# Second graph layer of a four-stage network on one core: slots per tile in place of the extra gathers

## The chip, the cores and the metric

One core of one Trainium2 chip runs the whole program. The metric is the device time of the program in microseconds, as the median of several executions. TensorE does matrix products, VectorE, ScalarE and GpSimd do elementwise work, SyncE issues transfers. In the profile they are PE (with PEld for its weight loads), DVE, ACT, POOL and SP.

## The reference, cut to what matters

The program is a graph layer, an expert layer, a second graph layer and a second expert layer over 3125 nodes of 256 features. The change concerns the sum over edges of the second graph layer. There are 103,125 edges, sorted by destination (`dst`), with a relation number each:

```python
h_src = h_hc[src]
r_uv = r_hc[edge_type]
m = clifford_linear(h_src * r_uv, msg_w, msg_b)
m = m * gate[:, :, None]
m = m * norm[:, None, None]
h_agg = jax.ops.segment_sum(m, dst, num_segments=num_nodes)
h_out = clifford_linear(h_hc + h_agg, upd_w, upd_b)
```

The linear map is taken out of the sum, so that the kernel sums products of a node's row and a relation's row, `h[src] * r[edge_type]`, over the edges of each destination. A 257th column carries the term of the bias.

## The kernel before, in words

**Tiles, blocks and halves.** The 3125 nodes lie in 25 tiles of 128 (`NT`). The sorted edges are cut into 404 blocks (`BLOCKS`) of two halves of 128 edges, 808 halves (`HALVES`). Each half is added to the tile in which its first edge lies. A half that begins in one tile and ends in a later one leaves out the edges behind the border. For these there are 24 extra halves (`EDGES_AT`), one for each tile from the second on, in 12 further blocks: the half in which that tile's first edge lies, this time with the weights of that tile. So `total` is 416 rounds.

**The loop, `aggregate` (lines 598 to 721).** Each engine runs over n from 0 to 415, and semaphores alone set the order:
- SyncE (L644) loads the 256 relation rows of block n into slot n mod 12 of `agg_r_rel` (`SLOTS` is 12). For the 12 extra rounds it reads two starts from the table `b_start` (L646) and loads 128 rows from each (L650).
- GpSimd (L659) gathers the 256 node rows with two indirect transfers of 128 rows into slot n mod 12 of `agg_r_rows`, by the table of sources `b_src`. It waits first until the sums of block n-12 are done, which used that slot (L656).
- ScalarE (L626, L629) makes a one-hot matrix per half from the distance of each edge's node to the tile's first (`b_near`).
- VectorE (L697) multiplies the gathered rows of both halves with the relation rows, in place. Then `add(n)` (L680 to L688) adds the two sums of block n-2 (`LAG` is 2) to the accumulator's tiles, whose numbers it reads from the table `b_tile` (L677). After each addition it waits for the one before (L686).
- TensorE (L715) multiplies each half's one-hot with its 128 x 257 products into one of six banks of PSUM, and counts `s_sum` up after the second. It waits for the product of round n, for the one-hot, and for the additions of block n-3, which free its banks.
- `beside` puts small work of the layer's end between the rounds, every 14th: transposes (L2512), a matmul (L2518), a copy by ScalarE (L2533) and two additions by VectorE (L2545, L2547).

`s_sum` begins at 13, from matmuls on zeros (L707), so that the waits of the first rounds pass. `s_sum >= n + 2` thus says that the sums of block n-12 are done.

**Tables.** `edge_blocks` (L436 to L578) makes `b_start`, `b_tile`, `b_src` and `b_near` at the start of the program and stores them. For the extra halves `b_start` holds the first edge of the half, a multiple of 128.

**The tile buffer.** `c.xn` (L2599, 25 x 256 numbers per partition) holds the normalised rows of each expert layer. It is free during `aggregate`.

## Time and profile before

| | us |
|---|---|
| median of 3 runs | 3672.89 |
| lowest and highest of the runs | 3659.75, 3688.53 |
| the profiled execution's own time | 3648.6 |
| its span, first to last instruction | 3646.8 |
| first gather to last addition of `aggregate` | 1873.9 to 3089.4 |

A row of the profile names the line, the engine, the operation and output<-inputs; then how often, and the time in us. "Idle before" is how long the engine had nothing to do before that row, with what ended it. "issue" stands for no wait that the profile shows, "remote" for an event that comes from no instruction or transfer of the profile. In a timeline a row begins with its start and its length in us from the span's start. The granted clock of TensorE is 1.0 at 2.4 GHz and 0.5 at 1.2 GHz.

### The profile page before, as it was taken

Reading aid. Unit: us, or ns where it says so; the run is one execution under the profiler, and the core shown is the slowest. Engines: PE = TensorE matmul, PEld = TensorE weight load, DVE = VectorE, ACT = ScalarE, POOL = GpSimd, SP = SyncE. Lnnn points to the kernel's source line nnn. Section 1 sums busy time; section 2 is a strip of 40 time slices with the busy share of each in tenths; the row PEclk is TensorE's granted clock in tenths of the full one; section 3 lists DMA queues with packets and bytes.
Section 4 is the critical chain, followed back from the end, with each engine's and each line's share of the span. In section 5 each row is a group of like instructions: output and inputs, shape, how many; then the busy total and the mean of one; then the engine's idle time right before and its main releaser. Section 6 shows DMA issues by size and latency. Waiting matters only on the chain. (4 is left out here: it accounts for less than half of the span.)

```text
span 3646.8 us, 47855 instructions
## 1 busy us (share of the span) xinstructions
PE 2327.2 (64%) x11533; PEld 1741.3 (48%) x11533; DVE 1680.2 (46%) x4536; ACT 1447.2 (40%) x3766; POOL 1987.8 (55%) x1945
## 2 busy tenths in 40 slices
PE   1658888957877745787115445544654455589997
PEld 1235556635555534666104233333333333579996
DVE  5656777735554623000455455544654555621110
ACT  0345556524443422222145334333433333345553
POOL 2546566555556457554537776776777765023332
PEclk9978999979978857999657767776766767799999
DMA  6646565555656565457346666666666664264232
GB/s 231 198 123 180 170 182 173 155 185 191 200 176 206 167 204 181 153 163 234 89 126 193 183 181 189 190 179 173 198 185 173 188 183 134 86 215 117 47 84 60
DMA packets 366569, 605.80 MB, mean 166 GB/s; under 512 B 82338, under 2 KB 235179, under 8 KB 363536
## 3 DMA queue, kind: packets, MB, share of 16 engines
q1 hardware_dynamic: 261984, 331.36, 28.2%
q0 software_dynamic: 100208, 265.56, 27.4%
q10 hardware_dynamic: 4144, 6.20, 0.5%
q8 instruction: 95, 1.56, 0.2%
q14 instruction: 138, 1.13, 0.1%
HBM read 443.45 MB, written 164.32 MB: 167 GB/s over the span
## 5 line engine op out<-in xcount | busy, mean ns | idle before, releaser
L659 POOL DMA_INDIRECT agg_r_rows<-h_table,parts_and_x x832 | 861.0, 1035 | 393.9 <-issue 232.5
L715 PE MATMUL agg_r_sums<-agg_r_rows,agg_r_onehot 128*128 128x257 f32 x1664 | 580.3, 493 | 598.2 <-issue 300.0
L715 PEld LDWEIGHTS agg_r_sums<-agg_r_rows,agg_r_onehot 128*128 128x128 f32 x1664 | 371.0, 241 | 794.4 <-issue 549.5
L688 DVE TENSOR_TENSOR acc<-acc,agg_r_sums 128x257 f32 (+1 forms) x836 | 353.6, 423 | 541.7 <-remote 347.4
L626 ACT ACTIVATE agg_r_gap<-iota,parts_and_x 128x128 f32<-128x128 f32 x832 | 286.0, 391 | 571.5 <-remote 330.2
L1558 POOL DMA_INDIRECT rl_buf<-r_table,kinds x312 | 336.2, 1078 | 247.7 <-DMA relation_rows<-rl_buf 150.6
L1388 PE MATMUL la_acc<-la_parts,la_counts 128*128 128x512 f32 x1250 | 342.6, 432 | 95.6 <-DVE la_parts L1471 38.3
L1558 POOL DMA_INDIRECT rm_buf<-r_table,kinds x280 | 270.3, 965 | 213.6 <-DMA relation_rows<-rm_buf 111.3
L1958 PE MATMUL f_pH<-f_xT,f_w 128*128 128x128 f32 x2816 | 350.6, 282 | 39.6 <-DMA f_w<-in_L_ffn_w 14.6
L1958 PEld LDWEIGHTS f_pH<-f_xT,f_w 128*128 128x128 f32 x2816 | 335.5, 196 | 72.5 <-issue 41.9
L1977 PE MATMUL f_pY<-f_w,f_hT 128*128 128x256 f32 x1408 | 333.5, 387 | 32.1 <-DMA f_w<-in_L_ffn_w 22.0
L1388 PEld LDWEIGHTS la_acc<-la_parts,la_counts 128*128 128x128 f32 x1250 | 253.0, 206 | 172.4 <-issue 84.5
L2043 ACT ACTIVATE f_hT<-f_pH,f_b 128x128 f32<-128x128 f32 x704 | 197.6, 372 | 333.2 <-PE f_pH L1958 332.8
L697 DVE TENSOR_TENSOR agg_r_rows<-agg_r_rows,agg_r_rel 128x514 f32<-128x514 f32 x416 | 287.8, 692 | 43.8 <-DMA agg_r_rows<-h_table,parts_and_x 32.6
L1977 PEld LDWEIGHTS f_pY<-f_w,f_hT 128*128 128x128 f32 x1408 | 262.6, 193 | 71.2 <-DMA f_w<-in_L_ffn_w 25.6
L1428 ACT ACTIVATE la_counts<-matrix 128x640 fp32r<-128x640 fp8e4 x250 | 180.9, 735 | 246.7 <-remote 98.1
L1154 PE MATMUL b_strips<-b_oh,b_at 128*128 128x400 bf16 x980 | 211.4, 349 | 93.8 <-issue 45.6
L2200 POOL DMA_INDIRECT f_xb<-xn_table,f_token x120 | 118.2, 985 | 257.7 <-DVE f_home L2148 124.8
L1275 DVE TENSOR_SCALAR b_oh<-b_numbers,b_code 128x400 bf16<-128x400 f16 x980 | 252.8, 324 | 0.0
L2188 POOL DMA_INDIRECT f_ys<-f_yb,f_home x56 | 88.2, 1575 | 270.5 <-DVE f_yb L2173 252.9
L2167 DVE TENSOR_TENSOR f_plain<-f_pY,f_b 128x256 f32<-128x256 f32 x56 | 23.8, 425 | 359.2 <-PE f_pY L1977 359.2
L629 ACT ACTIVATE agg_r_onehot<-agg_r_gap 128x256 f32<-128x256 f32 x416 | 173.3, 417 | 23.8 <-remote 8.2
(404 smaller groups left out, 3355.4 us busy)
## 6 DMA issues: line engine op xcount, KB each, us to landing
agg_r_rel<-relation_rows SPq DMA_DIRECT2D x404, 260.0 KB
relation_rows<-rl_buf SPq DMA_DIRECT2D x156, 260.0 KB
relation_rows<-rm_buf SPq DMA_DIRECT2D x140, 260.0 KB
relation_rows<-f_rr_buf POOLq DMA_DIRECT2D x60, 260.0 KB
f_w<-in_L_ffn_W SPq DMA_DIRECT2D x28, 512.0 KB
f_w<-in_L_ffn_W SPq DMA_DIRECT2D x14, 1024.0 KB
agg_r_rows<-h_table,parts_and_x POOLq DMA_INDIRECT x832
f_w<-in_L_ffn_w SPq DMA_DIRECT2D x38, 256.0 KB
```

What stands on the lines that cost most here:

```text
L626: last = nc.scalar.activation(gap[:, n % HOT, t, :], c.iota[:, 0:P], ACT.Abs, bias=c.tab["b_near"][:, bass.ds(g * 2 + t, 1)])
L659: pool.indirect_dma_start(rows[:, n % SLOTS, t, :], None, table, bass.IndirectOffsetOnAxis(ap=indices[:, t:t + 1], axis=0)).then_inc(s_row ...
L688: v.tensor_tensor(here, here, sums[:, (2 * (n - LAG) + t) % BANKS, 0:used], ALU.add).then_inc(s_acc, 1)
L697: v.tensor_tensor(here, here, rel[:, n % SLOTS, :, 0:used], ALU.mult).then_inc(s_ready, 1)
L715: last = nc.tensor.matmul(sums[:, (2 * n + t) % BANKS, 0:used], onehot[:, n % HOT, t, :], rows[:, n % SLOTS, t, 0:used], start=True, stop= ...
L1154: last = nc.tensor.matmul(strips[:, n % BANKS, 0:CODES], at[:, n % 2, t, :], oh[:, n % 2, t, :], start=t == 0, stop=t == DEEP - 1)
L1275: last = v.tensor_scalar(oh[:, n % 2, t, :], numbers[:, :], code[:, q, 1, own, t:t + 1], None, ALU.is_equal)
L1388: last = nc.tensor.matmul(acc[:, n % 2, :], counts[:, i, j, :], parts[:, s, :], start=s == 0, stop=s == NT - 1)
L1558: pool.indirect_dma_start(self.buf[:, n, g, :], None, self.table, bass.IndirectOffsetOnAxis(ap=self.c.kinds[:, at:at + 1], axis=0)).then_i ...
L1958: last = nc.tensor.matmul(pH[s][:, f * P:(f + 1) * P], w1b[:, s, f // (FC // 2), at:at + P], xT[:, s, h, :], start=h == 0, stop=h == KD - 1)
L1977: last = nc.tensor.matmul(pY[s][:, 0:D], hT[:, s, f, :], w2b[:, s, f, :], start=f == 0, stop=f == FC - 1)
L2043: nc.scalar.activation(hT[:, s, f, :], pH[s][:, f * P:(f + 1) * P], act_fn, bias=b1s[:, bass.ds(e, 1), f]).then_inc(s_hT, 1)
```

## The change

VectorE keeps each multiplied half in a slot of a new buffer, `c.saved`, that has one slot of 257 numbers for each of the 25 tiles and one spare. The slot's number is the tile of the half's first edge, so the last half that begins in a tile stays in its slot. That is the half that the extra sum of the next tile reads. The 12 extra rounds load, gather and multiply nothing. TensorE reads two table entries for each half (which half, and from `b_tile` its slot) and multiplies straight from the slot.

The copy stands in `add(n)`, ahead of each addition, and copies from the product of block n-2. So the gather's slot is free only after that copy: the limit in `gather` goes from `n + 2` to `n + 2 + BANKS // 2` (that is n + 5), the sums of block n-9. `c.xn` becomes a view of `c.saved`.

```diff
@@ tables
-                sp.dma_start(c.tab["b_start_d"], at[:, 0, :]).then_inc(s_saved, 16)
+                sp.dma_start(c.tab["b_start_d"], at[:, 1, :]).then_inc(s_saved, 16)
...
-                v.tensor_scalar(at[:, 0, :], starts, bits, bits, ALU.arith_shift_right, ALU.logical_shift_left)
@@ aggregate, SyncE
-                for n in range(BLOCKS, total):
-                    starts = [sp.value_load(c.tab["b_start"][0:1, at:at + 1], min_val=0, max_val=EDGE_TILES * P)
-                              for at in (2 * (n - BLOCKS), 2 * (n - BLOCKS) + 1)]
-                    sp.wait_ge(s_sum, n + 2)
-                    for t in range(2):
-                        sp.dma_start(rel[:, n % SLOTS, t, :], relation_rows[bass.ds(starts[t], P), :]).then_inc(s_rel[n % SLOTS], 16)
@@ GpSimd
-                    pool.wait_ge(s_sum, (n + 2))
+                    pool.wait_ge(s_sum, n + 2 + BANKS // 2)
...
-                for n in range(total):
+                for n in range(BLOCKS):
                     gather(n, c.tab["b_src"][:, n * 2:n * 2 + 2])
@@ VectorE, add(n)
                     for t in range(2):
+                        half = 2 * (n - LAG) + t
+                        if 0 <= half < HALVES:
+                            if half:
+                                dve.wait_ge(s_save, half)
+                            v.tensor_copy(saved[:, bass.ds(tiles[t], 1), :].rearrange("p a d -> p (a d)"), rows[:, (n - LAG) % SLOTS, t, 0:used])\
+                                .then_inc(s_save, 1)
                         dve.wait_ge(s_acc, 2 * n + t + BANKS)
@@ VectorE, the loop
+                    if n < BLOCKS:
-                    dve.wait_ge(s_rel[n % SLOTS], loads_of(n))
+                        dve.wait_ge(s_rel[n % SLOTS], (n // SLOTS + 1) * 16)
                         dve.wait_ge(s_rows[n % SLOTS], (n // SLOTS + 1) * 32)
                         here = rows[:, n % SLOTS, :, 0:used]
                         v.tensor_tensor(here, here, rel[:, n % SLOTS, :, 0:used], ALU.mult).then_inc(s_ready, 1)
                     add(n)
@@ TensorE
+                def slot_of(n, t):
+                    at = 2 * (n - BLOCKS) + t
+                    half = pe.value_load(c.tab["b_start"][0:1, at:at + 1], min_val=0, max_val=HALVES - 1)
+                    tile = pe.value_load(c.tab["b_tile"][0:1, bass.ds(half + 2 * LAG, 1)], min_val=0, max_val=NT)
+                    return saved[:, bass.ds(tile, 1), :].rearrange("p a d -> p (a d)")
+                def sum_up(n):
+                    terms = [rows[:, n % SLOTS, t, 0:used] if n < BLOCKS else slot_of(n, t) for t in range(2)]
                     pe.wait_ge(s_acc, 2 * (n + LAG + 1))
                     pe.wait_ge(s_oh, n + 1)
-                    pe.wait_ge(s_ready, g + 1)
+                    pe.wait_ge(s_ready, min(n + 1, BLOCKS))
+                    kept = HALVES if n >= BLOCKS else 2 * (n + 1 - BANKS // 2)
+                    if kept > 0:
+                        pe.wait_ge(s_save, kept)
                     for t in range(2):
+                        last = nc.tensor.matmul(sums[:, (2 * n + t) % BANKS, 0:used], onehot[:, n % HOT, t, :], terms[t], start=True, stop=True)
@@ build
-        c.xn = c.sb("xn", [P, NT, D])
+        c.saved = c.sb("saved", [P, (NT + 1) * (D + 1)])
+        c.xn = c.saved[:, 0:NT * D].rearrange("p (t d) -> p t d", d=D)
```

## Rows read from the trace of the kernel before

**Rows 1.** The page's costliest groups: the gathers, TensorE, VectorE in `aggregate`
```profile
L659 POOL DMA_INDIRECT agg_r_rows<-h_table,parts_and_x x832 | 861.0, 1035 | 393.9 <-issue 232.5
L715 PE MATMUL agg_r_sums<-agg_r_rows,agg_r_onehot 128*128 128x257 f32 x1664 | 580.3, 493 | 598.2 <-issue 300.0
L688 DVE TENSOR_TENSOR acc<-acc,agg_r_sums 128x257 f32 (+1 forms) x836 | 353.6, 423 | 541.7 <-remote 347.4
L697 DVE TENSOR_TENSOR agg_r_rows<-agg_r_rows,agg_r_rel 128x514 f32<-128x514 f32 x416 | 287.8, 692 | 43.8 <-DMA agg_r_rows<-h_table,parts_and_x 32.6
```

**Rows 2.** One line, L659: xcount, ns min/median/max, first and last start
```profile
L659 POOL DMA_INDIRECT agg_r_rows<-h_table,parts_and_x x832: 947/953/1463, 1873.9 to 3071.7; - x167
```

**Rows 3.** Waits of POOL in `aggregate`: us in total, times, longest
```profile
POOL agg_r_rows L659 <- issue: 232.5, 760, 0.9
POOL agg_r_rows L659 <- remote: 91.6, 43, 5.3
POOL agg_r_rows L659 <- PE agg_r_sums L707: 56.0, 1, 56.0
POOL agg_r_rows L659 <- PE agg_r_sums L715: 13.8, 28, 2.7
```

**Rows 4.** Timeline from 2402 us: quick rounds, all engines
```profile
2402.12 0.69 DVE L697 TENSOR_TENSOR agg_r_rows<-agg_r_rows,agg_r_rel 128x514 f32<-128x514 f32 x1
2402.36 1.27 POOL L659 DMA_INDIRECT agg_r_rows<-h_table,parts_and_x  x1 [0.30 <-PE agg_r_sums L715]
2402.77 0.99 DVE L688 TENSOR_TENSOR acc<-acc,agg_r_sums 128x257 f32 x2
...
2403.68 0.69 DVE L697 TENSOR_TENSOR agg_r_rows<-agg_r_rows,agg_r_rel 128x514 f32<-128x514 f32 x1
...
2403.94 1.26 POOL L659 DMA_INDIRECT agg_r_rows<-h_table,parts_and_x  x1 [0.30 <-issue]
```

**Rows 5.** Timeline of VectorE and GpSimd, 2310 to 2334 us: slow rounds
```profile
2310.65 0.69 DVE L697 TENSOR_TENSOR agg_r_rows<-agg_r_rows,agg_r_rel 128x514 f32<-128x514 f32 x1
...
2319.58 0.99 DVE L688 TENSOR_TENSOR acc<-acc,agg_r_sums 128x257 f32 x2 [8.23 <-issue]
...
2332.89 0.99 DVE L688 TENSOR_TENSOR acc<-acc,agg_r_sums 128x257 f32 x2 [11.72 <-remote]
...
2333.54 0.95 POOL L659 DMA_INDIRECT agg_r_rows<-h_table,parts_and_x  x1 [5.27 <-remote]
```

**Rows 6.** Timelines of DVE and of POOL, 110 to 124 us: one-input operations
```profile
114.91 7.27 DVE L959 TENSOR_SCALAR parts_and_x<-parts_and_x,ln_mean,ln_var 128x256 f32<-128x256 f32 x22
...
115.92 7.96 POOL L1558 DMA_INDIRECT r_buf<-r_table,kinds  x1 [0.30 <-issue]
```

**Rows 7.** Single lines L962 and L2541: a copy from SBUF, one from PSUM
```profile
L962 DVE COPY parts_and_x<-matrix x1: 281/281/281, 114.0 to 114.0; 1x256 f32<-1x256 f32 x1
...
L2541 DVE COPY g_offset<-be_result 128x256 f32<-128x256 f32 x1 | 0.4, 418 | 0.0
```

**Rows 8.** Timelines at the end of `aggregate`: last gathers, last rounds
```profile
3041.45 0.96 POOL L659 DMA_INDIRECT agg_r_rows<-h_table,parts_and_x  x1 [0.30 <-issue]
...
3071.75 0.95 POOL L659 DMA_INDIRECT agg_r_rows<-h_table,parts_and_x  x1 [0.31 <-issue]
...
3084.51 0.69 DVE L697 TENSOR_TENSOR agg_r_rows<-agg_r_rows,agg_r_rel 128x514 f32<-128x514 f32 x1
...
3085.91 0.69 DVE L697 TENSOR_TENSOR agg_r_rows<-agg_r_rows,agg_r_rel 128x514 f32<-128x514 f32 x1
3086.51 2.85 DVE L688 TENSOR_TENSOR acc<-acc,agg_r_sums 128x257 f32<-128x257 f32 x6
```

**Rows 9.** Single lines L646 and L1750: table reads by SP and by TensorE
```profile
L646 SPq TENSOR_LOAD <-parts_and_x x24: 3/268/705, 3025.6 to 3082.4; - x24
L646 SPq FUSED_REGOPS  x24: 3/152/713, 3025.9 to 3082.7; - x24
...
L1750 PEldq TENSOR_LOAD <-flags x1: 484/484/484, 1280.0 to 1280.0; - x1
L1750 PEldq FUSED_REGOPS  x1: 165/165/165, 1280.5 to 1280.5; - x1
```

More of the change, by code:

```diff
@@ L603, in aggregate @@
     total = BLOCKS + EDGES_AT // 2
+    saved = c.saved[:, :].rearrange("p (t d) -> p t d", d=used)
     with Core(nc) as k:
@@ L611, in aggregate @@
         s_rows = [c.pool_sem(f"{name}_rows{s}") for s in range(SLOTS)]
-        s_gap, s_oh, s_ready, s_sum, s_acc, s_gate = (k.sem(f"{name}_{x}") for x in (
-            "gap", "onehot", "ready", "sum", "acc", "gate"))
+        s_gap, s_oh, s_ready, s_save, s_sum, s_acc, s_gate = (k.sem(f"{name}_{x}") for x in (
+            "gap", "onehot", "ready", "save", "sum", "acc", "gate"))
         with nc.Block() as block:
@@ L667, in _ @@
                 v = nc.vector
-                def loads_of(n):
-                    slot = [q for q in range(n + 1) if q % SLOTS == n % SLOTS]
-                    return sum(16 if q < BLOCKS else 32 for q in slot)
                 def tile_of(half):
@@ L693, in _ @@
                 for n in range(total):
-                    dve.wait_ge(s_rel[n % SLOTS], loads_of(n))
-                    dve.wait_ge(s_rows[n % SLOTS], (n // SLOTS + 1) * 32)
-                    here = rows[:, n % SLOTS, :, 0:used]
-                    v.tensor_tensor(here, here, rel[:, n % SLOTS, :, 0:used], ALU.mult).then_inc(s_ready, 1)
+                    if n < BLOCKS:
+                        dve.wait_ge(s_rel[n % SLOTS], (n // SLOTS + 1) * 16)
+                        dve.wait_ge(s_rows[n % SLOTS], (n // SLOTS + 1) * 32)
+                        here = rows[:, n % SLOTS, :, 0:used]
+                        v.tensor_tensor(here, here, rel[:, n % SLOTS, :, 0:used], ALU.mult).then_inc(s_ready, 1)
                     add(n)
@@ L708, in _ @@
                 last.then_inc(s_sum, SLOTS + 1)
-                def sum_up(g, n):
-                    pe.wait_ge(s_acc, 2 * (g + LAG + 1))
-                    pe.wait_ge(s_oh, g + 1)
-                    pe.wait_ge(s_ready, g + 1)
+                def slot_of(n, t):
[5 more added lines that the diff above has]
+                    terms = [rows[:, n % SLOTS, t, 0:used] if n < BLOCKS else slot_of(n, t) for t in range(2)]
+                    pe.wait_ge(s_acc, 2 * (n + LAG + 1))
+                    pe.wait_ge(s_oh, n + 1)
+                    pe.wait_ge(s_ready, min(n + 1, BLOCKS))
+                    kept = HALVES if n >= BLOCKS else 2 * (n + 1 - BANKS // 2)
+                    if kept > 0:
+                        pe.wait_ge(s_save, kept)
                     for t in range(2):
-                        last = nc.tensor.matmul(sums[:, (2 * n + t) % BANKS, 0:used], onehot[:, n % HOT, t, :], rows[:, n % SLOTS, t, 0:used],
-                                                start=True, stop=True)
+                        last = nc.tensor.matmul(sums[:, (2 * n + t) % BANKS, 0:used], onehot[:, n % HOT, t, :], terms[t], start=True, stop=True)
                     last.then_inc(s_sum, 1)
                 for n in range(total):
-                    sum_up(n, n)
+                    sum_up(n)
                     beside.tensor(pe, n)
@@ L2598, in build @@
         crowded_gnn0(nc, c, I, edges, h_tables, x1, zh0)
-        c.xn = c.sb("xn", [P, NT, D])
+        c.saved = c.sb("xn", [P, (NT + 1) * (D + 1)])
+        c.xn = c.saved[:, 0:NT * D].rearrange("p (t d) -> p t d", d=D)
         logits = [c.sb(f"logits{q}", [P, NT, ne]) for q, ne in enumerate((E0, E1))]
```

## The prediction

> **What bounds the kernel now.** I read the page's groups first. In `aggregate` (1873.9 to 3089.4 us) no engine is full: GpSimd's gathers are busy 861.0 us, TensorE's products 580.3 us, VectorE's multiplications 287.8 us and additions 353.6 us [rows 1]. GpSimd is the nearest to full, so its waits come next. From the first gather's start to the last one's end are 3072.7 - 1873.9 = 1198.8 us [rows 2]. Of that 861.0 us are busy. The idle time is 393.9 us, of which 56.0 us lie ahead of the first gather [rows 1, 3], so 337.9 us are in the stage, and 861.0 + 337.9 is 1198.9: GpSimd's own account closes. The gap between two gathers with nothing to wait for is 0.30 us (232.5 us in 760) [rows 3]. 831 such gaps make about 252 us, which leaves 86 us of true waiting. The undisturbed gather takes 0.953 us, the median [rows 2]. 832 of them make 793 us, and the 68 us that are left are gathers that were held up.
>
> So the stage is GpSimd's: **793 + 252 + 68 held up + 86 waiting = 1199 us**, and behind it a tail of 16.7 us to the last addition (3089.4) [rows 8]. A round costs 1199 / 416 = 2.88 us, of which 2.51 us can't be had back while two gathers are made.
>
> What holds a gather up stands in the quick rounds. VectorE's round is 1.56 us (2402.12 to 2403.68). A gather that starts 0.24 us after a multiplication takes 1.27 us instead of 0.95, as if it had waited for the multiplication's end. The next starts 1.58 us later, again 0.26 us after a multiplication [rows 4]. Gathers and rounds run in step, so that nearly each gather loses 0.31 us. On the whole timeline 222 of the 416 rounds come in under 1.75 us, and 222 x 0.31 = 69 us is all of the held-up time.
>
> What makes GpSimd wait stands in the slow rounds. There VectorE stands 8 to 12 us before an addition, although the products it adds were issued long before, while GpSimd gathers on until the ring of 12 slots is full and it waits (5.27 us in the longest) [rows 5]. Just then the sums come through together. I count some 26 such endings. I can't say what delays the sums, but they cost only through GpSimd's 86 us.
>
> **The change part by part.**
>
> *The 24 gathers, 12 multiplications and 24 loads that go.* At the end GpSimd is the bound: the last gather of block 403 starts at 3041.45 and ends at 3042.4, the last of all ends at 3072.7, 24 gathers on [rows 8]. 24 x (0.953 + 0.303) = **-30 us**. The multiplications and loads lay beside that.
>
> *The 12 extra rounds are then a tail.* Before, the tail behind the last gather was 16.7 us. After it, the last gather must land and block 403 be multiplied, summed, copied and added two rounds later: some 7 us. Then come 12 rounds in which TensorE makes four table reads each. TensorE's only read in the trace took 0.484 us with 0.165 us of register work behind it; SyncE's took 0.268 and 0.152 us in the median [rows 9]. That is 0.42 to 0.65 us each, 1.7 to 2.6 us for four, one behind the other in its queue, and with the matmuls' own issue I take 2.7 us a round, near the upper row since it is the same engine. Were the reads hidden, a round would cost the 1.39 us at which the last rounds ran (3084.51 to 3085.91) [rows 8]. 7 + 12 x 2.7 + 3 for the last additions = 42 us, between 7 + 12 x 1.39 + 3 = 27 and, at 4 us a round, 58. Against 16.7 us: **+25 us** (+10 to +41).
>
> *The copies on VectorE.* 808 copies of 128 x 257. A copy of 256 numbers within SBUF took 0.281 us on one partition, one from PSUM 0.418 us [rows 7]; these are the bounds, and I take the first, since source and target are both in SBUF. With the address from a register and part of the second copy hidden in the gap between the additions, a quick round of 1.56 us becomes about 2.0 us (1.9 to 2.3). That is under the 2.51 us of two gathers, so VectorE does not become the bound: **0 us** directly. The cover is thin: a round of more than 2.5 us would put all beyond it on the path.
>
> *Gathers held up.* This decides. One row shows that VectorE's work with one input can shut a gather out: during 22 back-to-back L959 a gather took 7.96 us, until they were over [rows 6]. A copy can do that for its 0.28 us. Against it stands the lock step. If a gather that waited for a multiplication is let in at its end, it ends 0.83 us later, and the next starts at 0.69 + 0.83 + 0.30 = 1.82 us of a round that now has 2.0 us: ahead of the next multiplication. The step is broken, and gathers then meet a multiplication (0.69 us) or a copy (0.28 us) only by chance. Over 2.7 us of two gathers, that is (0.69² + 2 x 0.28²) / 2.7 = 0.24 us a round, or 404 x 0.24 = 95 us if each met part by chance alone; many fall into slow stretches without any, as now, and I take 78 us: **+10 us** (-40 if most are free; the upper bound is the first rival).
>
> The Trainium skill ("SBUF — State Buffer", section "Who interferes with whom") says that a VectorE copy in a two-port mode takes the port pair that GpSimd shares, for the whole instruction, while an operation with two SBUF inputs stops only GpSimd's reads. The trace agrees with 7.96 us under L959. By that rule every copy that meets a gather costs up to 0.28 us, 808 x 0.28 = 226 us at the very worst, where chance alone gives a tenth of it.
>
> *The shorter ring.* Gathers now wait for the sums of block n-9, not n-12. TensorE's new wait on the copies of block n-3 ends with the additions for which it waits anyway: 0 us. But three rounds of lead are gone: a slow stretch fills the ring after 3 x 2.51 = 7.5 us less. More endings, each with some 3.3 us of wait (86 / 26): between 18 and 38 of them, **+10 us** (-25 to +40).
>
> *The table, the larger buffer, one VectorE operation less* lie in other stages and off their paths: 0 us.
>
> Sum, against the profiled execution's own 3648.6 us: -30 + 25 + 10 + 10 = +15, about 3664 us. That execution stands 24 us under the median of the runs, so as a median **3688 us**.
>
> **The rivals.**
>
> *The lock step holds, at the longer round (slower).* If the first copy follows the multiplication without a gap in which a gather gets in, the gather is let in 0.94 us into the round, and the next starts at 0.94 + 0.83 + 0.30 = 2.07 us, just behind the next multiplication at 2.0. Then each gather of a quick stretch takes the whole 2.0 us, 0.74 us too much. VectorE's first addition starts 0.65 us after the multiplication's start, 0.04 us ahead of its end [rows 4], and 22 of L959 kept a gather out without letting it in between [rows 6], which speaks for it; that a wait and a register operation stand ahead of each copy speaks against. With 210 such gathers: 155 us, and 35 us by chance in the rest, against 68 now: +122 us, with the other terms (-30 + 25 + 10) +127, so 3800 us. With part of the gathers in step 3730 to 3760. It decides from the point where a round is shorter than 2.2 us.
>
> *The gathers come free (faster).* The step is broken, the quick stretches last longer, and GpSimd fills its ring more seldom: held-up time 30 us (-38), waiting 60 us (-26), tail at its lower bound (+10), gathers gone (-30): -84 us, 3590 us. For it: GpSimd with 0.95 us gathers in the slow rounds. Against: free gathers are also what leads to the full ring.
>
> *The tail and the ring alone (slower).* Table reads at 4 us a round (+41) and twice the endings (+86): with -30 and +10 that is +107, 3780 us. TensorE's single read is thin evidence, but two such misses at once are unlikely.
>
> *The change does not do what it says:* no sign of it; the slots' order and the waits cover the reads.
>
> **How the numbers follow.** My forecast (3640 to 3710) 0.43; the lock step, whole or in part, 0.32; tail and ring 0.08; gathers free 0.17. About 1% (37 us) is what a measurement here tells from no change. From the cases: faster by more 0.17, within 0.43, slower by more 0.40. The range for eight in ten is 3605 to 3800: it leaves out the far half of the free gathers and a lock step with further misses on top; the forecast's own is 3640 to 3710.
>
> **What would show it.** The gathers number 808. Median gather 0.95 us and mean 1.00 to 1.08: forecast; mean near 1.2, and timeline rows of POOL with 1.7 us at a distance of 2.0: lock step. The copy takes 0.28 us (0.42: VectorE's round passes 2.2 us, which also breaks the step). POOL's waits without the first stand under 150 us in "remote" and "PE". From the last gather to the last addition 27 to 58 us. I'm wrong if VectorE's quick round passes 2.5 us, or if the time moves outside `aggregate`.

## The result, and the profile after

The changed kernel takes 3693.19 us (median of 9 runs, 3669.74 to 3716.53), the kernel before in the same rounds 3672.89 us (3642.77 to 3698.35). The ratio is 1.0067 with a 95% interval of 1.0040 to 1.0095: 15 to 35 us more, within the 1% that was called no change. The forecast was 3688 us.

The page's costliest groups of the changed kernel, which answer to [rows 1]. The program allocates `c.saved` under the name `xn`, so `xn` in these rows is the new buffer:

```profile
L653 POOL DMA_INDIRECT agg_r_rows<-h_table,parts_and_x x808 | 791.7, 980 | 451.0 <-issue 221.3
L725 PE MATMUL agg_r_sums<-agg_r_rows,agg_r_onehot 128*128 128x257 f32 x1616 | 612.1, 528 | 550.2 <-DVE agg_r_rows L695 289.1
...
L680 DVE COPY xn<-agg_r_rows 128x257 f32 x808 | 271.2, 336 | 295.1 <-issue 217.3
L685 DVE TENSOR_TENSOR acc<-acc,agg_r_sums 128x257 f32 (+1 forms) x836 | 345.9, 414 | 110.4 <-issue 72.1
...
L695 DVE TENSOR_TENSOR agg_r_rows<-agg_r_rows,agg_r_rel 128x514 f32<-128x514 f32 x404 | 278.2, 689 | 32.1 <-issue 25.2
```

The single line of the gathers [rows 2], and GpSimd's waits in the stage [rows 3]:

```profile
L653 POOL DMA_INDIRECT agg_r_rows<-h_table,parts_and_x x808: 947/953/1474, 1890.8 to 3078.7; - x162
```

```profile
POOL agg_r_rows L653 <- issue: 221.3, 685, 3.2
POOL agg_r_rows L653 <- remote: 115.7, 50, 3.5
POOL agg_r_rows L653 <- PE agg_r_sums L725: 60.1, 72, 3.3
POOL agg_r_rows L653 <- PE agg_r_sums L705: 53.9, 1, 53.9
```

There are 24 gathers fewer, and the mean gather fell from 1035 to 980 ns: 791.7 - 808 x 0.953 leaves 22 us in which gathers were held up, where there were 68. But the idle time rose from 393.9 to 451.0 us. Without the 53.9 us ahead of the first gather and 807 gaps of 0.303 us (245 us), 153 us of true waiting are left, where there were 86. What was gained in the gathers went into waits.

A quick round is no longer in step with the gathers. The timeline of VectorE and GpSimd of the changed kernel from 2402.3 us, to be laid beside [rows 4]:

```profile
2402.30 0.69 DVE L695 TENSOR_TENSOR agg_r_rows<-agg_r_rows,agg_r_rel 128x514 f32<-128x514 f32 x1
...
2402.96 0.96 POOL L653 DMA_INDIRECT agg_r_rows<-h_table,parts_and_x  x1 [0.30 <-issue]
2402.97 0.32 DVE L680 COPY xn<-agg_r_rows 128x257 f32 x1
...
2403.21 0.41 DVE L685 TENSOR_TENSOR acc<-acc,agg_r_sums 128x257 f32 x1
...
2403.54 0.48 DVE L680 COPY xn<-agg_r_rows 128x257 f32 x1
...
2403.95 0.40 DVE L685 TENSOR_TENSOR acc<-acc,agg_r_sums 128x257 f32 x1
...
2404.22 0.95 POOL L653 DMA_INDIRECT agg_r_rows<-h_table,parts_and_x  x1 [0.30 <-issue]
2404.27 0.68 DVE L695 TENSOR_TENSOR agg_r_rows<-agg_r_rows,agg_r_rel 128x514 f32<-128x514 f32 x1
```

This round takes 1.97 us (2402.30 to 2404.27). The gathers keep their own beat of 1.26 us and run their 0.95 us.

Behind the last gather (end 3079.6 us) the 12 extra rounds are a tail, which ends with the last addition at 3131.9. The timeline of TensorE, VectorE and ScalarE in it:

```profile
3092.31 2.08 PE L725 MATMUL agg_r_sums<-xn,agg_r_onehot 128*128 x4 [3.08 <-DVE acc L685]
...
3094.43 0.88 DVE L685 TENSOR_TENSOR acc<-acc,agg_r_sums 128x257 f32<-128x257 f32 x2 [2.12 <-PE agg_r_sums L725]
...
3095.61 1.36 PEld L725 LDWEIGHTS agg_r_sums<-xn,agg_r_onehot 128*128 128x128 f32 x4 [1.94 <-issue]
3095.61 2.08 PE L725 MATMUL agg_r_sums<-xn,agg_r_onehot 128*128 x4 [1.23 <-ACT agg_r_onehot L629]
3097.73 0.69 ACT L626 ACTIVATE agg_r_gap<-iota,parts_and_x 128x128 f32<-128x128 f32 x2 [2.16 <-PE agg_r_sums L725]
3097.73 0.88 DVE L685 TENSOR_TENSOR acc<-acc,agg_r_sums 128x257 f32<-128x257 f32 x2 [2.42 <-PE agg_r_sums L725]
...
3098.91 2.07 PE L725 MATMUL agg_r_sums<-xn,agg_r_onehot 128*128 x4 [1.22 <-ACT agg_r_onehot L629]
```

The tail of 52.3 us has three parts: 12.7 us from the last gather's end to the first extra matmul (3092.31), 38.7 us of extra rounds, and 0.9 us to the end of the last addition. In the first part the five blocks still in the ring are multiplied, and at its end TensorE stands 3.08 us. In the extra rounds TensorE multiplies for 2.08 us, stands 1.23 us and multiplies again: 3.3 us a round, and VectorE and ScalarE wait for it. The rows name ScalarE's one-hot or an addition as what ended TensorE's wait. But ScalarE's last one-hot ends at 3112.1 us, and in the rounds behind it the gap is still 1.23 to 1.37 us. And the additions that TensorE waits for are those of block n-3, which are over by then. What fills the time are the table reads in TensorE's own queue, as the two single lines show (L711 reads the half, L712 the tile):

```profile
L711 PEldq TENSOR_LOAD <-parts_and_x x24: 296/300/316, 3088.3 to 3127.2; - x24
```

```profile
L712 PEldq TENSOR_LOAD <-b_tile x24: 300/305/318, 3089.1 to 3128.0; - x24
```

Lines of the same queue between 3095.7 and 3098.8 us, ahead of the round that starts at 3098.91, give their place in the round (the two reads of the half, and the register operations of the two reads of the tile):

```profile
L711 PEldq TENSOR_LOAD <-parts_and_x x2: 297/298/300, 3095.8 to 3097.2; - x2
L712 PEldq FUSED_REGOPS  x4: 46/98/151, 3096.4 to 3098.3; - x4
```

The first read starts 0.15 us after the round's first matmul (3095.61), while the matmuls run. The fourth read with its register work is over at 3098.5, and the next matmul starts 0.4 us later. So the four reads take 2.8 us with their register work, and 0.15 + 2.8 + 0.4 is the whole round. The matmuls lie beneath the reads, and the 1.23 us in which the engine stands is only what sticks out.

The stage from the first gather to the last addition, in the two profiled executions:

| | before | after | difference |
|---|---|---|---|
| gathers, undisturbed, with their gaps | 793 + 252 | 770 + 245 | -30 |
| gathers held up | 68 | 22 | -46 |
| GpSimd's waits | 86 | 153 | +67 |
| tail behind the last gather | 16.7 | 52.3 | +36 |
| stage | 1215.5 | 1241.2 | **+25.7** |

The last row is the measured loss; the rows above it are worked out with a mean gather and a mean gap and add up to it within 2 us. The profiled executions differ by more (3648.6 and 3691.8 us), and 16.9 us of it lie ahead of the stage, which starts at 1890.8 instead of 1873.9 us. That start is worth nothing here. In the profiles of the twelve experiments below it lies anywhere between 1862.9 and 1900.4 us, though ahead of the stage they differ by one small VectorE operation at most. So the runs give each kernel's time below, and the profile gives the length of the stage.

### The profile page after: what moved, and what is told of

It reads as the page before. It is cut to its first block and busy times, and to the rows that moved or that the text cites. A ratio compares the mean times of both kernels' runs of the same rounds, so it can differ in the third digit from the quotient of the medians.

```text
span 3689.9 us, 49872 instructions
## 1 busy us (share of the span) xinstructions
PE 2390.1 (65%) x11533; PEld 1769.1 (48%) x11534; DVE 1853.4 (50%) x5331; ACT 1448.0 (39%) x3766; POOL 1913.3 (52%) x1921
## 3 DMA queue, kind: packets, MB, share of 16 engines
q8 instruction: 98, 1.61, 0.2%
## 5 line engine op out<-in xcount | busy, mean ns | idle before, releaser
L653 POOL DMA_INDIRECT agg_r_rows<-h_table,parts_and_x x808 | 791.7, 980 | 451.0 <-issue 221.3
L725 PE MATMUL agg_r_sums<-agg_r_rows,agg_r_onehot 128*128 128x257 f32 x1616 | 612.1, 528 | 550.2 <-DVE agg_r_rows L695 289.1
L725 PEld LDWEIGHTS agg_r_sums<-agg_r_rows,agg_r_onehot 128*128 128x128 f32 x1616 | 381.1, 259 | 768.8 <-issue 539.7
L680 DVE COPY xn<-agg_r_rows 128x257 f32 x808 | 271.2, 336 | 295.1 <-issue 217.3
L685 DVE TENSOR_TENSOR acc<-acc,agg_r_sums 128x257 f32 (+1 forms) x836 | 345.9, 414 | 110.4 <-issue 72.1
L695 DVE TENSOR_TENSOR agg_r_rows<-agg_r_rows,agg_r_rel 128x514 f32<-128x514 f32 x404 | 278.2, 689 | 32.1 <-issue 25.2
```

Source lines behind the costliest of these rows:

```text
L653: pool.indirect_dma_start(rows[:, n % SLOTS, t, :], None, table, bass.IndirectOffsetOnAxis(ap=indices[:, t:t + 1], axis=0)).then_inc(s_row ...
L680: v.tensor_copy(saved[:, bass.ds(tiles[t], 1), :].rearrange("p a d -> p (a d)"), rows[:, (n - LAG) % SLOTS, t, 0:used])\
L685: v.tensor_tensor(here, here, sums[:, (2 * (n - LAG) + t) % BANKS, 0:used], ALU.add).then_inc(s_acc, 1)
L695: v.tensor_tensor(here, here, rel[:, n % SLOTS, :, 0:used], ALU.mult).then_inc(s_ready, 1)
L725: last = nc.tensor.matmul(sums[:, (2 * n + t) % BANKS, 0:used], onehot[:, n % HOT, t, :], terms[t], start=True, stop=True)
```

## The experiments

My first reading of the two profiles was this (theory A in the expectations): the copies break the lock step, which frees 46 us, and the shorter ring costs 67 us of waits. It was tested first.

The table has all kernels. "To the last gather" counts from the first one's start, "held up" and "waits" are worked out as above, and "quick" is the median round of those under 2.3 us, from one multiplication's start to the next. The ratio compares a kernel with runs of the kernel before that were taken beside it. Every other column comes from one profiled execution.

| kernel | ratio to before (95%) | to last gather | tail | stage | held up | waits | quick |
|---|---|---|---|---|---|---|---|
| before | 1 | 1198.8 | 16.7 | 1215.5 | 68 | 86 | 1.57 |
| after | 1.0067 (1.0040 to 1.0095) | 1188.9 | 52.3 | 1241.2 | 22 | 153 | 1.87 |
| e1 ring of 9 | 0.9988 (0.9961 to 1.0014) | 1205.1 | 10.4 | 1215.5 | 58 | 103 | 1.57 |
| e2 copies alone | 1.0051 (1.0025 to 1.0076) | 1214.1 | 16.0 | 1230.1 | 29 | 140 | 1.82 |
| e3 gathers back | 1.0052 (1.0021 to 1.0082) | 1224.3 | 10.6 | 1235.0 | 20 | 160 | 1.87 |
| e4 ring by copy, two waits | 1.0147 (1.0104 to 1.0190) | 1213.8 | 61.6 | 1275.3 | 16 | 184 | 1.87 |
| e5 narrow copies | 1.0024 (1.0002 to 1.0046) | 1209.1 | 16.5 | 1225.6 | 67 | 97 | 1.61 |
| e6 double copies | 1.0191 (1.0163 to 1.0220) | 1276.4 | 11.7 | 1288.1 | 162 | 70 | 2.08 |
| e7 ring by copy, one wait | 1.0158 (1.0133 to 1.0184) | 1216.0 | 61.9 | 1277.8 | 16 | 185 | 1.87 |
| e8 pause | 0.9989 (0.9962 to 1.0016) | 1208.4 | 10.6 | 1219.1 | 69 | 95 | 1.57 |
| e9 reads ahead | 0.9987 (0.9963 to 1.0011) | 1188.3 | 27.3 | 1215.5 | 27 | 146 | 1.87 |
| e10 no copies | 1.0010 (0.9984 to 1.0037) | 1169.2 | 47.2 | 1216.4 | 74 | 81 | 1.57 |
| e11 no extra rounds | 0.9915 (0.9888 to 0.9943) | 1166.5 | 18.8 | 1185.3 | 61 | 91 | 1.57 |
| e12 stored by DMA | 1.0048 (1.0018 to 1.0078) | 1175.2 | 48.0 | 1223.2 | 39 | 122 | 1.95 |

### e1_ring9: the shorter ring alone

```diff
-                    pool.wait_ge(s_sum, (n + 2))
+                    pool.wait_ge(s_sum, n + 2 + BANKS // 2)
```

> The kernel before with one edit: gather n waits until block n-9 is summed instead of n-12; no copies, gathers of the extra rounds kept. Theory A (the two profiles put side by side): of the changed kernel's aggregate, POOL's waits grew by about 66 us because its ring is shorter, whatever VectorE does. Then this kernel takes about 60 us more than the kernel before (3710 to 3750), the time that gathers are held up stays near 68 us, and POOL's waits are near 150 us. Theory B (the longer waits come from VectorE's longer rounds, the copies in them): this kernel is within 15 us of the kernel before, with POOL's waits near 86 us.

Theory A falls. The median is 3658.9 us against 3660.91 us, and the stage is 1215.5 us, the very length of before. GpSimd's waits rose from 86 to 103 us, a quarter of what I had put down to the ring and little more than e8's 95 with the ring of before, and the tail was 6 us shorter (e8, with the ring of 12, has 10.6 us, so it says nothing). Theory B's number for the time held.

### e2_copies: the copies alone

```diff
+                        half = 2 * (n - LAG) + t
+                        if 0 <= half < HALVES:
+                            if half:
+                                dve.wait_ge(s_save, half)
+                            v.tensor_copy(c.xn[:, half % NT, :], c.h[:, half % NT, :]).then_inc(s_save, 1)
                         dve.wait_ge(s_acc, 2 * n + t + BANKS)
```

> The kernel before with a copy of 128x256 ahead of each addition, from node rows that nothing writes to a tile that nothing reads, so ring, gathers and tail are as before. Theory A: the copies lengthen a quick round from 1.56 us to about 1.8 us, gathers no longer start right behind a multiplication, and the time held up falls from 68 to about 22 us with POOL's waits unchanged: 30 to 50 us less than the kernel before. Theory B (the copies are what makes POOL wait): 20 to 60 us more, POOL's waits near 150 us.

GpSimd's gathers and waits in it (page, then waits):

```profile
L659 POOL DMA_INDIRECT agg_r_rows<-h_table,parts_and_x x832 | 821.9, 988 | 447.5 <-issue 224.4
```

```profile
POOL agg_r_rows L659 <- remote: 114.6, 52, 4.9
POOL agg_r_rows L659 <- PE agg_r_sums L711: 55.3, 1, 55.3
POOL agg_r_rows L659 <- PE agg_r_sums L719: 53.2, 44, 3.4
```

The full ring of 12 is there, nothing is gathered less, and still the pattern is that of the changed kernel: held up 29 us (-39), waits 140 us (+54). Theory A was right on the first number and wrong on the second, so the kernel is slower, by 0.51% (19 us; the stage by 14.6 us), at the low end of theory B. The waits come with the copies, not with the ring.

### e3_gathers_back: copies and ring, without the tail

```diff
-                for n in range(BLOCKS):
+                for n in range(total):
                     gather(n, c.tab["b_src"][:, n * 2:n * 2 + 2])
...
-                    terms = [rows[:, n % SLOTS, t, 0:used] if n < BLOCKS else slot_of(n, t) for t in range(2)]
+                    terms = [rows[:, n % SLOTS, t, 0:used] for t in range(2)]
```

> The changed kernel with the 24 extra gathers (and their relation rows and multiplications) back; copies and the ring's limit of the changed kernel kept. Theory A: 24 gathers cost 24 x 1.25 = 30 us and the tail falls from 52 to about 17 us, so it is 0 to 15 us below the changed kernel. Theory B (the tail is the whole loss): 35 us below it. If the copies' mere presence is the loss, the same as the changed kernel or above it.

The stage is 1235.0 us, 6.2 us under the changed kernel's: until the last gather it is 35.4 us longer, and its tail is 41.7 us shorter. The two nearly cancel, as expected, and 19.5 us of the loss remain with the copies.

### e10_no_copies: gathers and tail, without the copies

```diff
-                            if half:
-                                dve.wait_ge(s_save, half)
-                            v.tensor_copy(saved[:, bass.ds(tiles[t], 1), :].rearrange("p a d -> p (a d)"), rows[:, (n - LAG) % SLOTS, t, 0:used])\
-                                .then_inc(s_save, 1)
...
-                    pool.wait_ge(s_sum, n + 2 + BANKS // 2)
+                    pool.wait_ge(s_sum, n + 2)
```

> The changed kernel without the copies and without their waits, with the gather's limit of the kernel before (block n-12). The extra sums read the slots as they lie, so what they add is left out of the reference's sums. This is the edit of the gathers and the tail alone. From the stages of e3_gathers_back and the changed kernel (35 us less until the last gather, 42 us more behind it): 0 to 15 us over the kernel before, and 10 to 25 us below the changed kernel. If copies and tail were tied together (a cost that comes only with both), it is below the kernel before.

It is the mirror of e3: 1.0010, stage 1216.4 us. Until the last gather 29.6 us went, and the tail grew by 30.5 us. Held-up time (74) and waits (81) are back at their values of before. So the change splits: gathers and tail +0.9 us, and the rest +24.8 us (1241.2 - 1216.4). That rest is the copies together with the shorter ring and TensorE's wait on the copies; e1 gives the ring alone as nothing, and e2 the copies alone as 14.6 us; what makes up the 10 us between these is not shown.

### e5_narrow and e6_double: the dose

```diff
-                            v.tensor_copy(c.xn[:, half % NT, :], c.h[:, half % NT, :]).then_inc(s_save, 1)
+                            v.tensor_copy(c.xn[:, half % NT, 0:16], c.h[:, half % NT, 0:16]).then_inc(s_save, 1)
```

```diff
-                            v.tensor_copy(c.xn[:, half % NT, :], c.h[:, half % NT, :]).then_inc(s_save, 1)
+                            v.tensor_copy(c.xn[:, half % NT, :], c.h[:, half % NT, :])
+                            v.tensor_copy(c.xn[:, (half + 5) % NT, :], c.h[:, (half + 5) % NT, :]).then_inc(s_save, 1)
```

> As e2_copies, but each copy is 128x16 instead of 128x256: the same instructions, waits and semaphore increments, little of the time on VectorE. Theory C (what the copies cost is VectorE's time in the quick rounds: the stage ran 14.6 us longer in e2_copies with a quick round of 1.87 us): the quick round is about 1.65 to 1.7 us and the stage 0 to 6 us over the kernel before. Theory D (the cost is one more semaphore and two more instructions per half, or that any delay breaks the lock step of gathers and multiplications): the stage is 12 to 20 us longer, as in e2_copies, and POOL's waits over 130 us.

> As e2_copies, with two copies of 128x256 for each half in place of one. Theory C: the quick round comes to about 2.4 us, near the 2.5 us in which POOL gathers a block, hardly anything is caught up after a slow stretch, and the stage is 40 us or more over the kernel before. Theory D: no more than e2_copies, 12 to 20 us.

The narrow copies leave the pattern of before (held up 67, waits 97, against 69 and 95 in e8), and the quick round is 1.61 us, under the 1.65 to 1.7 that was expected. So theory D's sign, waits over 130 us from any added instruction, did not come. Their 0.24% (interval 0.02% to 0.46%) lies between the two forecasts, and the stage's +10 us with it, so a small cost of the instructions themselves stays possible. Double copies cost 72.6 us in the stage, over theory C's 40 and far over theory D's 20. But they cost it by another way than theory C said. The quick round is 2.08 us, not 2.4, and the waits fell to 70 us, below those of before. The timeline of e6_double at 2037 us:

```profile
2037.46 0.68 DVE L702 TENSOR_TENSOR agg_r_rows<-agg_r_rows,agg_r_rel 128x514 f32<-128x514 f32 x1
2037.63 1.77 POOL L659 DMA_INDIRECT agg_r_rows<-h_table,parts_and_x  x1 [0.30 <-PE agg_r_sums L720]
2038.06 0.28 DVE L689 COPY xn<-h 128x256 f32<-128x256 f32 x1
...
2038.27 0.28 DVE L690 COPY xn<-h 128x256 f32<-128x256 f32 x1
...
2038.47 0.41 DVE L693 TENSOR_TENSOR acc<-acc,agg_r_sums 128x257 f32 x1
...
2038.80 0.28 DVE L689 COPY xn<-h 128x256 f32<-128x256 f32 x1
...
2039.54 0.68 DVE L702 TENSOR_TENSOR agg_r_rows<-agg_r_rows,agg_r_rel 128x514 f32<-128x514 f32 x1
2039.71 1.77 POOL L659 DMA_INDIRECT agg_r_rows<-h_table,parts_and_x  x1 [0.30 <-PE agg_r_sums L720]
```

The gather starts 0.17 us after the multiplication and ends 1.77 us later, 0.82 us longer than an undisturbed one. Its end lies 0.85 us behind the second copy's (2038.55). In the kernel before, a gather that met a multiplication ended 0.82 us behind the multiplication [rows 4], so here the two copies shut it out as well. The next one starts 2.08 us later, once more 0.17 us after a multiplication. This is the first rival's lock step at the longer round, with its arithmetic: 154 gathers of this kernel took over 1.5 us, and none did in before, after or e2_copies. It takes two copies back to back. In the changed kernel 45 gathers started in the first 0.45 us of a multiplication with one copy right behind it, and in the median they too ended 0.82 us behind the multiplication (e2: 42 gathers, 0.83 us). The single copy cost them nothing. Why two do is not shown.

### e4_ring_by_copy and e7_ring_save: the ring given back by the copies

```diff
-                    pool.wait_ge(s_sum, n + 2 + BANKS // 2)
+                    pool.wait_ge(s_sum, n + 2)
+                    if n >= SLOTS:
+                        pool.wait_ge(s_save, 2 * (n - SLOTS + 1))
```

> The changed kernel with one edit: gather n waits on POOL for the sum of block n-12 and for that block's copies (made in round n-10), instead of for the sum of block n-9. The ring is then one to two blocks longer. Theory A (the ring is the price): POOL's waits fall from about 150 us by 20 to 45 us, and the time with them; held-up time stays near 22 us: 3650 to 3675. Theory B (the ring's length is no matter): within 10 us of the changed kernel.

The opposite came: 3722.89 us, stage 34 us longer than the changed kernel's. I suspected the second wait on GpSimd, and e7_ring_save has only one:

```diff
-                    pool.wait_ge(s_sum, n + 2 + BANKS // 2)
+                    if n < SLOTS:
+                        pool.wait_ge(s_sum, n + 2)
+                    else:
+                        pool.wait_ge(s_save, 2 * (n - SLOTS + 1))
```

> The changed kernel with the gather's wait on the sum of block n-9 replaced by one wait on the copies of block n-12 (from block 12 on): e4_ring_by_copy without its second wait on POOL. If e4's loss of some 30 us on the changed kernel came from the second wait on POOL, this one takes the changed kernel's time or up to 20 us less; if it comes from where in the round the ring is released (the copies, in VectorE's order, in place of the sum), it takes as long as e4, 3715 to 3730.

It takes as long as e4 (3718.77 us, stage 1277.8 us), so the second wait cost nothing. The wait named in its waits view is the copies':

```profile
POOL agg_r_rows L656 <- DVE xn L683: 195.4, 100, 6.2
```

A ring that is a block or two longer in count is worse here, because its release sits behind VectorE's own wait. In the changed kernel GpSimd is let go by TensorE's sum, in e7 by the copy two rounds behind, which in a slow stretch itself stands until a sum comes through. The idle times of over 1 us ahead of a gather are 64 instead of 72, but less the usual gap 2.8 us long in the mean instead of 2.0, and rounds of over 5 us number 86 instead of 56. At the last gather's end nine blocks are left to multiply instead of five, which makes the tail 9.6 us longer. The numbers are measured; that the order of VectorE's queue makes them is argued.

### e8_pause: a pause on GpSimd

```diff
                     pool.sem_inc(s_gate, 1)
+                    nc.gpsimd.memset(still[:, n:n + 1], 0.0)
```

> The kernel before with one 128x1 memset on POOL ahead of each block's two gathers, a pause of a few tenths of a microsecond per block. Theory E (the sums' increments reach the other engines late while gathers run without a break, and short breaks let them through): POOL's waits fall by as much as the memsets add or more, and the time is at or below that of the kernel before. Theory F (POOL's time bounds the stage): 416 pauses of 0.1 to 0.3 us, 40 to 125 us more, POOL's waits unchanged near 86 us.

The time is that of the kernel before, 0.9989. This tells nothing between the theories, because there was no pause. The memset's single line:

```profile
L659 POOL MEMSET agg_r_still<- x416: 98/117/125, 1897.1 to 3103.7; 128x1 f32 x139
```

It takes 0.117 us in the median, and with it in between, the distance from a gather's end to the next gather's start is still 0.305 us: it fits into the gap that was there. So the kernel serves as a repeat of before instead: its stage of 1219.1 us against 1215.5 us says that such lengths come again within some 4 us, and its waits of 95 against 86 us that these come again within some 9 us.

### e9_hoist: TensorE's table reads ahead of the tail

```diff
                 for n in range(total):
                     sum_up(n)
                     beside.tensor(pe, n)
+                    if BLOCKS - EDGES_AT <= n < BLOCKS:
+                        at = n - (BLOCKS - EDGES_AT)
+                        slots[at] = slot_of(BLOCKS + at // 2, at % 2)
```

> The changed kernel with TensorE's 48 table reads of the 24 extra sums made in the last 24 blocks' rounds, one pair behind each block's matmuls, instead of ahead of each extra round. Theory G (an extra round is 2.1 us of matmuls and 1.2 us of table reads, one behind the other): the extra rounds fall from 3.3 to about 2.1 us, the tail from 52 to 36 to 40 us, and the time by 12 to 16 us. Rival (VectorE's additions or ScalarE's one-hot rows are next in the tail's chain at nearly the same rate): the tail falls by under 5 us.

The stage is back at 1215.5 us, and the ratio to before is 0.9987 against the changed kernel's 1.0067. The tail fell by 25 us, well over theory G's 12 to 16, and the extra rounds alone from 38.7 to 12.65 us. Two rows of the windows view show them, first 38 us of the changed kernel's, then all of e9_hoist's (window, length, busy us and count of PE, PEld, DVE, ACT, POOL, then the granted clock, DMA share and GB/s):

```profile
3092.00:3130.00 38.00, 23.91 (x47) 13.80 (x48) 9.60 (x23) 6.66 (x18) 0.00 (x0) 0.50 0.00 0
```

```profile
3101.00:3115.00 14.00, 12.65 (x48) 9.94 (x48) 9.98 (x25) 6.33 (x18) 0.00 (x0) 0.88 0.00 1
```

The first window ends within the last round; all 48 matmuls are busy 24.9 us in the changed kernel (12 x 2.08) and 12.65 us here. Theory G added matmuls and reads, one behind the other. But the reads ran beside the matmuls and took 2.8 us of each round by themselves, so taking them away took away what set the round. Without them TensorE multiplies without a break. The granted clock, 0.50 throughout the changed kernel's extra rounds (its lower level, 1.2 GHz), is 0.88 in the mean here. Where it is 0.50 (3102.4 to 3105.8 us) TensorE's round is 1.71 us, where it is 1.00 it is 0.87 us, until VectorE's two additions set the pace at 0.97 us; they now follow one another:

```profile
3106.18 6.79 DVE L685 TENSOR_TENSOR acc<-acc,agg_r_sums 128x257 f32<-128x257 f32 x14 [0.64 <-PE agg_r_sums L725]
```

At 1.71 us throughout, the 12 rounds would have taken some 20 us. So by this estimate some 8 us of the 26 came with the clock and the others with the reads. That the gaps held the clock down is likely, because nothing else was changed, but in the changed kernel the clock cost nothing there: the matmuls at 2.08 us fitted under the reads. The reads themselves cost nothing where they went (1188.3 us to the last gather, against 1188.9 in the changed kernel).

### e11_no_extra and e12_stored: how much there is to win

```diff
-    total = BLOCKS + EDGES_AT // 2
+    total = BLOCKS
```

> The kernel before without its 12 extra rounds (24 gathers, multiplications and sums are left out of the computation): what the extra sums cost in all in the kernel before, and so the most that any way of making them can bring. If POOL's rate is what they take, 24 gathers x 1.25 to 1.45 us: 30 to 35 us less. If the stage is set by the slow rounds, 12 rounds x 2.9 us, the same 35 us. If they were hidden, under 15 us.

All 12 extra rounds of the kernel before cost 30.2 us of the stage, 0.85% of the time. That is the 24 gathers at the end, as the forecast had them, and it is the most that any other way of making the sums can bring.

```diff
+                def store(m):
+                    sp.wait_ge(s_ready, m + 1)
+                    dst = products[m * BLOCK:(m + 1) * BLOCK, :].rearrange("(k p) c -> p k c", p=P)
+                    sp.dma_start(dst, rows[:, m % SLOTS, :, 0:used]).then_inc(s_out[m % SLOTS], 16)
...
-                        sp.dma_start(rel[:, n % SLOTS, t, :], relation_rows[bass.ds(starts[t], P), :]).then_inc(s_rel[n % SLOTS], 16)
+                        sp.dma_start(rows[:, n % SLOTS, t, 0:used], products[bass.ds(starts[t], P), :]).then_inc(s_back[n % SLOTS], 16)
...
+                    if n >= SLOTS:
+                        pool.wait_ge(s_out[n % SLOTS], 16 * (n // SLOTS))
```

> A way of keeping the products that takes nothing from VectorE: the kernel before, with SyncE storing each multiplied block to a DRAM tensor by DMA (263 KB a block, 106 MB in all) and reading the 24 halves back for the extra sums, which then need neither a gather nor a multiplication. Gather n also waits for the store of block n-12. If VectorE's time is what the copies cost, the quick round stays at 1.57 us and the stage falls below the kernel before by 5 to 25 us (35 us of gathers gone, 10 to 30 us of tail come). If the extra DMA traffic is in the way of the gathers' landing or of the ring's release, it is 20 us or more above it.

Neither side came. It is 0.48% slower (the two medians lie closer, 3667.40 against 3659.43 us), the stage 7.7 us longer, and the quick round grew to 1.95 us with no copy in it. The windows view of the kernel before and of e12_stored over the same stretch, columns as above:

```profile
1900.00:3040.00 1140.00, 590.16 (x1764) 391.66 (x1763) 595.90 (x1246) 446.97 (x1262) 815.89 (x787) 0.71 0.66 185
```

```profile
1900.00:3040.00 1140.00, 623.68 (x1731) 402.41 (x1729) 584.94 (x1218) 436.88 (x1236) 782.47 (x782) 0.70 0.91 272
```

The DMA engines are 91% busy instead of 66% and move 272 GB/s instead of 185. The round is longer although VectorE does no more, and again held-up time is down (39 for 68) and the waits are up (122 for 86). Whether the waits come from the longer round or from the fuller DMA engines this run can't tell. The stores themselves hardly hold GpSimd up, for their 60 times are no longer than the usual gap of 0.30 us:

```profile
POOL agg_r_rows L676 <- DMA agg_r_products<-agg_r_rows: 18.3, 60, 0.3
```

## Why the prediction was right, and where its steps were not

The time was right, 3693 for 3688 us, and the class too. The forecast's +15 us stands against +25.7 us in the stage. Of its five terms one was right, the tail was too small, the one for held-up gathers had the wrong sign, and the waits came out at 67 us for 10 and from the copies, which the sum had at nothing. That the total was close is luck in good part.

*The 24 gathers.* Forecast -30, measured -29.6 (e10) and, with the sums gone as well, -30.2 us (e11). Right, and for the reason given: at the end GpSimd is the bound.

*The tail.* Forecast 42 us at 2.7 us a round, measured 52.3 us at 3.3. The upper end of 58 held. Part by part, 7 us until the first extra round became 12.7, the 32 us of 12 rounds became 38.7, and 3 us for the last additions became 0.9. The first part was too small because five blocks were still to be multiplied, and TensorE stood 3.08 us before its first extra matmul (in e9, where it stood 2.98 us, the row names VectorE's copy as what ended it; in e10, without copies, it stood 1.99 us). So TensorE's new wait, set at 0 us, has a part in this once. In the rounds the structure was right, the reads one behind the other set them, but the four take 2.8 us with their register work for the forecast's 1.7 to 2.6, and 0.5 us of waits and issue come on top.

*The copies.* "0 us directly" is the step that failed. The duration was right (0.28 us at the least, 336 ns in the mean, for 0.281), so was the quick round (1.87 us, forecast 2.0 with 1.9 to 2.3), and it is well below the 2.51 us of two gathers. From this I concluded that VectorE's time costs nothing while it stays below GpSimd's. e2 (+14.6), e3 (+19.5), the changed kernel against e10 (+24.8) and e6 (+72.6) say that it does. VectorE did not become the bound; the cost came through GpSimd's waits (e2: +54 us, with 39 us fewer held up), and the sum had no such term for the copies.

*Gathers held up.* Forecast +10, measured -46 us: the step was broken as drawn, but then hardly any gather was held up. The lock step arithmetic was sound, the chance arithmetic behind it, 78 us, was far above the 22 us that came: 74 of 808 gathers took over 1.05 us, where 231 of 832 did before. Free gathers were the second rival, which had 30 us held up. The signs named for the forecast failed too: a mean gather of 1.00 to 1.08 us (it is 0.980) and GpSimd's waits under 150 us in "remote" and "PE" (115.7 + 60.1). The Trainium skill ("SBUF — State Buffer", section "Who interferes with whom") lets a copy hold GpSimd off for its whole length. e6 agrees for two copies in a row behind a multiplication; with one copy per half no such cost shows, since the held-up time fell. The row of [rows 6] is a weaker witness than it was taken for: the 7.96 us gather ended at 123.88, 1.7 us after the last L959 but 0.83 us after the L964 behind them, an operation with two inputs. So that operation held it too.

*The shorter ring.* Forecast +10 us of waits with a range up to +40, and +67 came, nearly all from something else. e1 gives the ring alone as nil in the stage and +17 us in the waits. The copies bring them: e2 has +54 us of waits with the ring of 12. That they do it through the longer quick round is likely, and e12 fits, with +36 us at a quick round of 1.95 us and no copy, but its DMA engines are fuller too. "Free gathers are also what leads to the full ring", the point against the second rival, was the right sentence, and it should have been a term of the sum. Held-up time and waits together were forecast at +20 us and came to +21 us, by two errors that happen to cancel: -46 for +10 and +67 for +10.

*The rivals.* The lock step at the longer round was given 0.32 and decided on whether a gather gets in between a multiplication and the first copy. With one copy per half the gather is not kept out any longer, and with two it is, which e6 shows at 2.08 us a round and 1.77 us a gather; the mechanism was real and the point from which it decides was misplaced. Gathers that come free happened in the held-up time alone. Its 60 us of waits came out as 153.

*What stays open.* What delays the sums in the slow stretches, and why these come sooner after a longer quick round, was not settled. All kernels have 50 to 86 rounds of over 5 us, and e8, which was to touch this, made no pause. In the kernel before, the products that ended at 2305.9, 2313.5 and 2323.4 us were all counted only at 2332.8 us, where VectorE went on [rows 5]. That the copies cost time is shown by adding them, by taking them out, and by their dose (stages +10, +15 and +73 us for narrow, whole and double copies). The step from a longer round to more waits is argued: the waits do not rise with the round throughout (e6 has the longest quick round and 70 us), only where the gathers run free.

## What to carry to other kernels

Time that an engine spends below the bound's period need not be free where a ring is filled by one engine and emptied in bursts by the others: here 0.3 us more in a quick round of 1.57 us, against a period of 2.51 us, came with 46 us less of held-up gathers and 67 us more of waits. Price it by a dose (none, a sliver, one, two) before calling it covered. When work is moved behind the last transfer it becomes a tail at the speed of its slowest chain: look there for scalar reads in the queue ahead of the matmuls and make them earlier. Size them by the queue's own time (2.8 us a round here) and not by the gap that they leave on the engine (1.23 us). A ring's depth in blocks mattered less here than who releases it: nine slots freed by the sum were as good as twelve, and twelve freed by the next engine down the line were worse.

## What the runs showed of the hardware that was not expected

- Four table reads by TensorE's queue took 2.8 us (0.30 us for each read, the rest register work), and they ran beside the matmuls of the round before: 2.08 us of matmuls lay beneath them, and the engine showed a gap of 1.23 us only.
- The granted clock of the extra rounds was 0.50 with these gaps between groups of four matmuls, and 0.88 in the mean once they were gone; the 48 matmuls were busy 24.9 and 12.65 us. Taking out 11 gaps, some 14 us, shortened the rounds by 26 us.
- A 128x1 memset of 0.117 us on GpSimd between two gathers cost nothing: from one gather's end to the next one's start there were 0.305 us with it and without it.
- A second wait on GpSimd ahead of each block, mostly satisfied already, cost nothing that shows (e4 against e7, stages of 1275.3 and 1277.8 us).
- A multiplication with two copies behind it makes a gather 1.77 - 0.95 = 0.82 us longer, although a semaphore wait stands ahead of each pair of copies; with one copy right behind, 45 gathers ended 0.82 us behind the multiplication, as with none.
- The start of the stage lay between 1862.9 and 1900.4 us in fourteen profiled executions whose kernels are alike up to there but for one small VectorE operation. With effects of under 1%, two profiled spans can't be compared; two stages can.
